# Decoder layers on one core: feed-forward weights split early and parked in DRAM

## The reference

```python
x = x + attention(layernorm(x))             # 16 heads of 64, causal
x = x + cross_attention(layernorm(x), ctx)  # 16 heads of 16, linear: K^T V first, then Q (K^T V)
x = x + ffn(layernorm(x))                   # two layers l = 0, 1, each as below

def ffn_layer(x):
    h = shift_token(x)                      # upper half of the features from the token before
    q, k, v = split(h @ wqkv[l], 3)         # 256 x 1536, 8 heads of 64
    q = rotary(l2norm(q) * q_scale[l]); k = rotary(l2norm(k) * k_scale[l])
    x = x + local_attention(q, k, v) @ wo[l]   # windows of 128, own and previous window
    h = layernorm(shift_token(x)) * ln_g[l] + ln_b[l]
    a, g = split(h @ w1[l] + b1[l], 2)      # 256 x 1364
    return x + (a * gelu(g)) @ w2[l] + b2[l]
```

## Time and profile before

| what | before |
|---|---|
| median of 3 runs (lowest, highest) | 1188.23 us (1187.99, 1189.28) |
| the profiled execution: own time | 1190.71 us |
| the profiled execution: span of its instructions | 1188.9 us |
| granted TensorE clock, mean | 0.995 of full speed |
| busy: TensorE / VectorE / ScalarE / GpSimd | 96% / 69% / 58% / 48% |
| DMA: moved, mean busy share of 16 engines (q1) | 46.14 MB, 13.1% |

### The profile page before, as it was taken

The page is one execution under the profiler, slowest core; times in us unless marked ns, Lnnn a source line. Parts: engine busy times, 40 slices in busy tenths (PEclk is TensorE's granted clock), DMA queues, the critical chain, the costliest instruction groups (busy, mean ns, idle before and its releaser), DMA issues.

```text
span 1188.9 us, 19605 instructions
## 1 busy us (share of the span) xinstructions
PE 1138.9 (96%) x6624; PEld 886.1 (75%) x6624; DVE 816.7 (69%) x2443; ACT 692.5 (58%) x1696; POOL 567.4 (48%) x618
## 2 busy tenths in 40 slices
PE   4999999999999999998989999999999999999998
PEld 3778778787877766766667777777877778777686
DVE  5878778778877456689988566766575765654541
ACT  2677677777677223453676646747565565573821
POOL 2344544444454222148976464655554646561520
PEclk9999999999999999999999999999999999999999
DMA  7122221312121500011030000000001000001010
GB/s 238 41 50 62 56 50 41 80 37 54 41 50 40 174 18 18 1 62 36 2 131 1 1 1 18 2 1 1 1 18 48 27 1 1 1 16 57 18 36 18
DMA packets 30273, 46.14 MB, mean 39 GB/s; under 512 B 4576, under 2 KB 18016, under 8 KB 30176
## 3 DMA queue, kind: packets, MB, share of 16 engines
q1 hardware_dynamic: 30176, 44.90, 13.1%
HBM read 23.92 MB, written 4.19 MB: 24 GB/s over the span
## 4 chain that ended last, share of the span: by engine, by line
PE 86%; DVE 6%; ACT 3%; issue 2%; POOL 1%; DMA 0%; DVEq 0%; ACTq 0%; POOLq 0%
PE psum L1483 53%; PE psum L1572 6%; PE psum L1554 5%; PE psum L1704 5%; PE psum L1753 5%; PE psum L1738 5%; PE psum L1720 4%; PE psum L1686 2%; ACT hnT_hi L955 1%; ACT hnT L955 1%; DVE stats L1027 1%; PE psum L1766 1%; DVE rb L1272 1%; DVE y L1036 0%; DVE ss L1276 0%
## 5 line engine op out<-in xcount | busy, mean ns | idle before, releaser
L688 POOL TENSOR_TENSOR probs<-probs,rden 128x128 f32<-128x128 f32 (+3 forms) x256 | 176.5, 721 | 195.9 <-DVE rden L1094 195.9
L925 ACT ACTIVATE lp<-lp,lneg,rn 128x256 f32<-128x256 f32 (+1 forms) x256 | 143.8, 572 | 20.3 <-DVE lneg L1323 20.1
L837 ACT ACTIVATE probs<-probs,negmax 128x128 f32<-128x128 f32 (+3 forms) x256 | 140.7, 551 | 15.1 <-DVE negmax L1089 14.5
L1082 DVE CUSTOM_DVE_ANT_0 probs<-psum,causal 128x512 f32<-128x512 f32 (+3 forms) x256 | 110.0, 487 | 13.3 <-PE psum L1483 13.3
L727 POOL TENSOR_TENSOR rn<-ssm,neg_half 128x8 f32<-128x8 f32 x64 | 106.1, 1657 | 0.0
L1311 DVE CUSTOM_DVE_ANT_0 lp<-psum,local 128x256 f32<-128x256 f32 (+1 forms) x256 | 84.2, 385 | 22.0 <-PE psum L1704 21.9
L718 POOL TENSOR_TENSOR lp<-lp,lrden 128x768 f32<-128x768 f32 x64 | 94.9, 1483 | 0.0
L1483 PE MATMUL psum<-w,hid 124*128 124x256 f32 (+2 forms) x384 | 87.4, 385 | 2.6 <-DVE hid L1387 2.6
L1554 PE MATMUL psum<-ident,probs 128*128 128x128 f32 x640 | 86.0, 273 | 1.5 <-DVE pT L1103 1.1
L1483 PE MATMUL psum<-q,k_rest 128*128 128x256 f32 (+2 forms) x256 | 85.5, 345 | 1.3 <-DVE rowmax L1082 1.0
L1483 PEld LDWEIGHTS psum<-w,hid 124*128 124x128 f32 (+2 forms) x384 | 73.2, 193 | 14.4 <-issue 4.0
(11 more groups left out here) (167 smaller groups left out, 2982.2 us busy)
## 6 DMA issues: line engine op xcount, KB each, us to landing
k<-k_round SPq DMA_DIRECT2D x128, 128.0 KB, 2.4
x<-in_x SPq DMA_DIRECT2D x8, 512.0 KB, 6.3
aw<-in_w_quads SPq DMA_DIRECT2D x4, 768.0 KB, 4.7
w_raw<-in_w SPq DMA_DIRECT2D x2, 1364.0 KB, 6.4
ctxT<-in_ctxT SPq DMA_DIRECT2D x4, 512.0 KB, 7.3
x_scratch<-x SPq DMA_DIRECT2D x4, 512.0 KB, 2.9
x<-x_scratch SPq DMA_DIRECT2D x4, 512.0 KB, 6.3
wqkv_raw<-in_wqkv SPq DMA_DIRECT2D x1, 1536.0 KB, 10.2
```

The lines of the kernel that those rows point to most:

```text
L688: ins = pool.tensor_tensor(pr, pr, rden[:, u % 2, h, i:i + 1].broadcast_to([P, TRI[i]]), ALU.mult)
L837: ins = act.activation(pr, pr, ACT.Exp, bias=negmax[:, u % 2, h, i:i + 1], scale=ADH ** -0.5, accum_out=den[:, u % 2, h, i:i + 1])
L925: ins = act.activation(pr, pr, ACT.Exp, bias=lneg[:, u % 2, h, w:w + 1], scale=rn[:, m % 2, w, 0, 2 * j + h:2 * j + h + 1], accum_out=lden ...
L1082: ins = dve.tensor_tensor_reduce(probs[:, u % 2, h, TRI_AT[i]:TRI_AT[i + 1]], bank[:, at:at + TRI[i]], causal[:, S - TRI[i]:S], 1.0, -3e38 ...
```

## The change

**Splitting moves into the self-attention units.** All feed-forward weights are laid out on the host as one array `w_all` of 8360 columns a layer by 128 rows (wqkv in three parts, w1, w2, wo). It is cut into 11 parts of 760 columns a layer, 22 in all. In units 4 to 25 each part goes through the same path: SyncE loads it (`load_part`), ScalarE rounds it (`round_part`, item `part` behind `pk`), GpSimd subtracts in place (`rest_of_part`, item `part` behind the second `f`), SyncE stores both halves to a scratch array in DRAM (`store_part`), and waits for the stores before it loads the part after next.

**The halves are read back ready for use.** `layer_wqkv_lo`, `layer_wqkv_hi` and `layer_w1` load both halves from DRAM; `weights`, `w1_parts`, and their VectorE and ScalarE work in entry and steps are gone. TensorE waits for the loads instead. w2 and wo are still loaded unsplit, though their columns are split too.

**Tables.** `tab.0` moves to VectorE's unit 28 and `tab.1` behind the second cross-attention norm; both are stored to DRAM and each layer's one is loaded into a single `tab`, layer 1's after the last q and k tile of layer 0. The buffers of all this lie in `y`, which is free until the cross-attention ends.

**Orders.** `START_*`, `ENTRY_*` and `CLOSE_*` are rewritten on all engines; of these tables the diff shows one pair of lines. The repeated unit differs by the `part` items alone, the step by the missing ones.

```diff
+W_SIZE = (E2 * INNER,) * 3 + (E2 * 2 * HID, NF * D, FPAIRS * D)
+W_AT = [sum(W_SIZE[:i]) for i in range(len(W_SIZE) + 1)]
+W_PARTS = 11
+FIRST_PART = 4
+W_PART = W_AT[-1] // W_PARTS
...
+        w_raw = sbt(raw, "w_raw", [P, 2, W_PART])
+        w_half = sbt(raw, "w_half", [P, 2, W_PART], F32R)
...
+        w_rest = sbt(raw, "w_rest", [P, 2, W_PART], F32R)
...
-        START_PE = ("xT.0 pq.0 pk.0 pv.0 xT.1 s.0.0 s.0.1 pk.1 xT.2 pq.1 pv.1 t.0.0 pv.2 s.1.0 t.0.1 "
+        START_PE = ("xT.0 pv.0 xT.1 pk.0 pq.0 pv.1 s.0.0 s.0.1 pk.1 pq.1 pv.2 t.0.0 t.0.1 xT.2 s.1.0 "
...
-        UNIT_ACT = ("t1 e0@1 pk@2 t3 t5 aw0 pq@2 aw1 e1@1 pv@2 aw2")
-        UNIT_POOL = ("f0@6 f1@6")
+        UNIT_ACT = ("t1 e0@1 pk@2 part t3 t5 aw0 pq@2 aw1 e1@1 pv@2 aw2")
+        UNIT_POOL = ("f0@6 f1@6 part@6")
...
+                if what == "part" and 0 <= n - FIRST_PART < DEPTH * W_PARTS:
+                    items.append((what, n - FIRST_PART))
...
+            def store_part(i):
+                l, c = divmod(i, W_PARTS)
+                sp.wait_ge(part_lo, i + 1)
+                for half, tile in enumerate((w_half, w_rest)):
+                    sp.dma_start(w_dram[l, half, :, c * W_PART:(c + 1) * W_PART], tile[:, i % 2, :].bitcast(F32))\
+                        .then_inc(part_st, 16)
...
+                i = u - FIRST_PART - 2
+                if 0 <= i < DEPTH * W_PARTS:
+                    store_part(i)
+                    if i + 2 < DEPTH * W_PARTS:
+                        sp.wait_ge(part_st, 2 * 16 * (i + 1))
+                        load_part(i + 2)
...
-            wait_early(sp)
+            sp.wait_ge(l_tab, 6 * DEPTH)
+            for l, done in enumerate((tab_first, rot)):
+                sp.dma_start(tab_dram[l], done[:, :, :, :].rearrange("p a t d -> p (a t d)")).then_inc(tab_st, 16)
+            sp.wait_ge(tab_st, 16 * DEPTH)
+            wait_full(sp, plan["awo", B - 1, 1])
+            for c in range(3):
+                layer_wqkv_hi(0, c)
+            wait_read(sp, plan["kv", B - 1, T - 1])
+            layer_tab(0)
...
+            wait_full(sp, plan["q", B - 1, T - 1])
+            layer_wqkv_lo(1, 0)
+            layer_wqkv_hi(1, 0)
...
+            def rest_of_part(i):
+
+                pool.wait_ge(part_hi, i + 1)
+                pool.tensor_tensor(w_rest[:, i % 2, :], w_raw[:, i % 2, :], w_half[:, i % 2, :], ALU.subtract)\
+                    .then_inc(part_lo, 1)
...
-            def round_weights(l):
-
-                act.wait_ge(ld_wqkv, 16 * (1 + 3 * l))
...
+            def round_part(i):
+
+                act.wait_ge(ld_part[i % 2], 16 * (i // 2 + 1))
+                if i >= 2:
+                    act.wait_ge(part_st, 2 * 16 * (i - 1))
+                copy(w_half[:, i % 2, :], w_raw[:, i % 2, :]).then_inc(part_hi, 1)
...
                     if m % B == 0:
-                        pe.wait_ge(w_lo, 3 * l + "qkv".index(what) + 1)
+                        pe.wait_ge(ld_wqkv["qkv".index(what)], 2 * 16 * (l + 1))
```

More of the change, by code:

```diff
@@ L81, in constants, with build @@
             "c_rot": np.ascontiguousarray(rot)}
-def build(nc, a, out, x2_dram):
+def build(nc, a, out, x2_dram, w_dram, tab_dram):
     with ExitStack() as ctx:
@@ L101, in build @@
         k_rest = sbt(raw, "k_rest", [P, 2, S], F32R)
+        w_raw = sbt(raw, "w_raw", [P, 2, W_PART])
+        w_half = sbt(raw, "w_half", [P, 2, W_PART], F32R)
+        raw.close()
+        raw = ExitStack()
+        k_rest_again = sbt(raw, "k_rest_again", [P, 2, S], F32R)
+        w_rest = sbt(raw, "w_rest", [P, 2, W_PART], F32R)
+        raw.close()
+        raw = ExitStack()
+        k_rest_too = sbt(raw, "k_rest_too", [P, 2, S], F32R)
+        rot = sbt(raw, "rot", [P, 4, T, FDH])
+        tab_first = sbt(raw, "tab_first", [P, 4, T, FDH])
+        qk_scale = sbt(raw, "qk_scale", [P, DEPTH, 2, FDH])
         raw.close()
@@ L107, in build @@
         raw.close()
[L108 to L111, removed]
+        wqkv_lo = sbt(ctx, "wqkv_lo", [P, 3, E2, INNER], F32R)
         stats = sbt(ctx, "stats", [P, 2, T, 12])
@@ L210, in build @@
         raw.close()
-        wqkv_hi = sbt(ctx, "wqkv_hi", [P, E2, 3 * INNER], F32R)
+        wqkv_hi = sbt(ctx, "wqkv_hi", [P, 3, E2, INNER], F32R)
         sq = sbt(ctx, "sq", [P, 2, INNER])
-        tab = [sbt(ctx, f"tab{l}", [P, 4, T, FDH]) for l in range(DEPTH)]
-        rot = tab[DEPTH - 1]
-        qk_scale = sbt(ctx, "qk_scale", [P, DEPTH, 2, FDH])
+        tab = sbt(ctx, "tab", [P, 4, T, FDH])
         hT_hi = sbt(ctx, "hT_hi", [P, E2, S + 1], F32R)
@@ L251, in build @@
         x2_st = sem("x2_st")
-        ld_rot, ld_small, ld_wqkv, ld_lwo, ld_w1, ld_w2 = (
-            sem(n) for n in ("ld_rot", "ld_small", "ld_wqkv", "ld_lwo", "ld_w1", "ld_w2"))
+        ld_rot, ld_small, ld_lwo, ld_w1, ld_w2 = (
+            sem(n) for n in ("ld_rot", "ld_small", "ld_lwo", "ld_w1", "ld_w2"))
+        ld_wqkv = [sem(f"ld_w{what}") for what in "qkv"]
+        ld_tab, tab_st = sem("ld_tab"), sem("tab_st")
+        ld_part = [sem(f"ld_part{i}") for i in range(2)]
+        part_hi, part_lo, part_st = sem("part_hi"), sem("part_lo"), sem("part_st")
         set1 = sem("set1")
         ld_shift = sem("ld_shift")
-        w_hi, w_lo = sem("w_hi"), sem("w_lo")
         hid_one, last_gate = sem("hid_one"), sem("last_gate")
-        w1_hi_ok, w1_lo_ok = sem("w1_hi_ok"), sem("w1_lo_ok")
         hn_hi, hn_lo = sem("hn_hi"), sem("hn_lo")
@@ L399, in step_items @@
                     items.append((what, n))
-                if what == "weights" and n == B:
-                    items.append((what, 1))
-                if what == "tab" and n == B:
-                    items.append((what, 1))
-                if what == "wparts" and n % B == 0:
-                    items.append(("w1_parts", n // B))
             return items
@@ L774, in _ @@
                     probabilities(*at)
+                if what == "part":
+                    rest_of_part(*at)
                 if what == "norm2":
@@ L779, in _ @@
                     query_norms(*at)
-                if what == "weights" and at[0] == 0:
+                if what == "zeros":
                     set_zeros()
@@ L938, in evac_O @@
                 copy(loT[:, FPAIRS - 1 - u % FPAIRS, :], bank[:, :]).then_inc(read[use[0]], 1)
-            def split_w1(l):
-                act.wait_ge(ld_w1, 16 * (l + 1))
-                for e in range(E2):
-                    copy(w1_hi[:, e, :], w1_raw[:, e, :]).then_inc(w1_hi_ok, 1)
             def evac_hnT(m):
@@ L996, in _ @@
                     evac_xo(*at)
-                if what == "weights":
-                    round_weights(*at)
-                if what == "w1_parts":
-                    split_w1(*at)
+                if what == "part":
+                    round_part(*at)
                 if what == "hT":
@@ L1229, in tables @@
                 H = FDH // 2
+                dst = (tab_first, rot)[l]
                 for i in range(2):
@@ L1432, in _ @@
                 if what == "y":
+                    if at[0] == 0:
+                        dve.wait_ge(tab_st, 16 * DEPTH)
                     norm_apply(norm_no["y", at[0]], x[:, at[0]], y[:, at[0]])
-                if what == "weights":
-                    rest_of_weights(*at)
-                if what == "w1_parts":
-                    rest_of_w1(*at)
                 if what == "tab":
@@ L1670, in qkv_tile @@
                     if m % B == 0:
-                        pe.wait_ge(w_lo, 3 * l + "qkv".index(what) + 1)
+                        pe.wait_ge(ld_wqkv["qkv".index(what)], 2 * 16 * (l + 1))
                 use = plan[what, m, t]
                 bank = wait_free(pe, use)
-                cols = slice("qkv".index(what) * INNER, ("qkv".index(what) + 1) * INNER)
+                c = "qkv".index(what)
                 rows = slice(t * P, (t + 1) * P)
-                product(bank[:, :], [(h[:, e, rows], w[:, e, cols]) for e in range(E2)
+                product(bank[:, :], [(h[:, e, rows], w[:, c, e, :]) for e in range(E2)
                                      for h, w in ((hT_lo, wqkv_hi), (hT_hi, wqkv_lo), (hT_hi, wqkv_hi))])\
@@ L1898, in by_hidden_tiles, with by_partitions, rows @@
         return tiles
+    def by_partitions(wqkv, w1, w2, wo):
+        def rows(w):
+            w = np.asarray(w)
+            return w.reshape(DEPTH, -1, P, w.shape[-1]).transpose(0, 2, 1, 3).reshape(DEPTH, P, -1)
+        qkv = [rows(np.asarray(wqkv)[..., c * INNER:(c + 1) * INNER]) for c in range(3)]
+        return np.concatenate(qkv + [rows(w1), w2.reshape(DEPTH, P, -1), rows(wo)], -1)
     arrays = {
```

146 lines of the change are left out of this document (71 added, 75 removed), and 89 rows, old and new, of tables (CLOSE_DVE, ENTRY_ACT, ENTRY_DVE, ENTRY_PE).

## The result

| | before | after |
|---|---|---|
| median, us (runs) | 1188.76 (4) | 1203.11 (4) |
| lowest to highest | 1187.99 to 1189.83 | 1201.91 to 1204.84 |
| profiled execution: own time, span | 1190.7, 1188.9 | 1201.95, 1200.2 |

The changed kernel takes 1.0117 times as long, 95% interval 1.0105 to 1.0129. The prediction said 8.7 us faster; it is 14.4 us slower by the medians, 11.3 by the spans of the two profiled executions.

What follows compares the result with a forecast made beforehand. TensorE, busy nearly all the span, was taken as the bound, waiting in the entry for VectorE's chain. Terms -9.0 - 1.6 - 1.0 + 1.1 + 1.8 = -8.7 us gave 1179.5 us from the median of 1188.2, range 1172 to 1189.

Steps and rivals of the forecast that it cites:

- SyncE and DMA: Units: two stores and a load per part between copies of k on SyncE's queue, taken to cost 0.
- Rival 3: Copies of k queue behind the parts on SyncE in each of 22 units: about 1214 us, chance 0.06.
- Entry: Up to 650 us: 7.7 us leaving VectorE taken back, plus 1.3 behind: -9.0 us, bounds 0 and -13.7.
- clock's 1.4: Entry: one window where the granted clock fell to 0.71 would be 1.4 us shorter at full clock.
- Rival 2: GpSimd takes VectorE's place in the entry, only 3 of the 9 us come: 1185.5 us, chance 0.10.
- Tables: Two rotary tables, 2.7 us of VectorE each at most, in their new places: 0, at most +2.
- Units: 22 parts: +1.1 us, ScalarE's copies ending 0.06 ahead of z's start; three units also splitting a quad's weights: +1.8 us.
- Rival 1: Path ScalarE, GpSimd, TensorE late in every unit, 0.4 us each, 8.8 in place of 1.1: 1187.2 us, chance 0.15.
- rival 4: Nine aw_lo in three quad units each held for a whole 1.81 us GpSimd subtraction: 1194 us, chance 0.03.
- Layer 1: Split of layer 1's weights, between steps 1 and 2, replaced by loads: -1.6 us, range 0 to -1.6.
- Start: From 25 to 105 us: pv.0 goes first and fills a wait: -1.0 us, from +2 to -3.7.
- Rival 5: Halves return from DRAM too late for the first q tile, entry's gain gone: 1188.5 us, chance 0.04.

Runs made afterwards that it cites:

- e1: Changed kernel with SyncE's block that stores and loads a part put ahead of the wait for aw_lo and the quad's load: 1190.7 us, 1.0015 times before.
- e6: Changed kernel with the next part's load ahead of the aw_lo wait, then the quad's load, then stores, with no wait for stores just issued: 1193.5 us.
- e7: e5 with the entry's four lists of the kernel before, less the splits' items, both tables behind norm2.1: 1191.9 us.
- e5: Changed kernel with e1's edit and tab.0 moved behind norm2.1: 1189.3 us, ratio 1.0001 to the kernel before.
- e9: e5 with 16 parts (w2, wo unsplit), none in units that split aw, and the close's lists of the kernel before: 1184.4 us, 0.9947 times before.
- e10: e5 with 16 parts (w2, wo unsplit), none in units splitting aw, and the start's old lists, part.0 kept in GpSimd's: 1189.2 us.
- e2: Changed kernel with the quad's load still first, no wait for stores just issued, each part's load one unit later: 1205.3 us.

## Why the prediction was wrong

*SyncE and DMA, "0": this term failed.* Rival 3 had the right mechanism, copies of k queued behind the parts on SyncE, but I set its condition with the times of a plain unit: stores and load between 235.45 and 244.3. In a plain unit that held, stores landed in 2.6 and 3.3 us and loads in 3.1, and no copy of k was late. In the two units with a quad's load the term of the order was missing: SyncE first waits for `aw_lo` until some 2 us before the source of the next copies is ready (114.36 and 116.56), and 768 KB stand ahead of the stores. The stores then took 6.0 and 6.4 us. The low end of that reading, the load landing at 242, has no row behind it; loads of a part landed in 3.1 us. I had costed these units on ScalarE and VectorE only (+1.8, measured +1.5), never on the queue. Price: 12.4 us by e1, of which e6 gives 9.7 to the wait and 2.8 to the bytes. The prediction's own test, "DMA as what it waits for at scores", is what the profile showed.

*Entry, -9.0: right in sign, -5.7 measured.* The step that failed is "I take back the 7.7 us that leave VectorE". Taken out under the old order they gave 1.9 us (e7), 1.1 of it in idle time. A nearly full engine is not the bound if the waits at which TensorE stands are chains through it with gaps elsewhere. I named the new order in half a sentence and gave it nothing; it gave 2.3 in idle time. The "clock's 1.4" came in this execution, partly by luck: three of ten executions with the new lists still have the fall. Rival 2 was partly there: with the old order the wait for GpSimd's rotation grew from 2.5 to 2.9 us, a small part of the 6 us that rival took away, and the new order cut it to 0.5.

*Tables, "0, at most +2": +2.2.* I gave a table "2.7 us of VectorE each at most"; tab.0 took 3.6. "Go where TensorE is gapless and VectorE three quarters busy" was an argument from shares. The place in the list counts: ahead of the copies of t.28, and beside GpSimd's f. Behind norm2.1 the same table takes 1.5 us and costs nothing in the traces (e5).

*Close, "0, within 1 either way": +2.0,* the new order of the close (e9).

*Units, +1.1 and +1.8:* right, +1.2 and +1.5. `w_half` took 826 ns and `w_rest` 1834, against 0.83 and 1.81 us forecast. GpSimd's f was waited for twice, 0.6 us each, in units 14 and 22 only. Rival 1 did not come at its price, but its path was met: z waits 0.07 us for ScalarE's copies in every other plain unit. The "0.06 ahead" was no slack: where z waits, it starts 0.36 us behind the end of those copies.

*The port pair (rival 4): its price did not come in its place, but leaving it without a term was wrong.* The median of aw_lo is 698 ns (688 before). The first aw_lo of each of the three quads took 1.31 or 1.32 us already before (three in twelve, where the prediction counts one), and 1.32, 0.97 and 0.97 after. The rule of the Trainium skill (SBUF — State Buffer, SBUF: two separate sides) fits these and, better, tab.0, whose instructions have two SBUF inputs: 3.6 us beside GpSimd's f instead of 1.5, ahead of what TensorE waits for. In e10 a `negmax` with one SBUF input ends with the subtraction of a part, 1.23 us instead of 0.17, and that costs 1.1. Both are holds on TensorE's path, which the prediction sought at aw_lo alone.

*Layer 1, -1.6:* right. The first hidden products of steps 1 and 2, in the chain of waits of the kernel after, against the earlier trace rows:

```profile
737.77 2.97 PE psum L1512 x12
...
816.10 2.97 PE psum L1512 x12
```

78.3 us apart, where it had been 79.9. *Start, -1.0:* right in size (0.4 to 1.8 by the traces). *Rival 5* did not come: no wait for the layers' halves shows.

The forecast's sum of right terms was thus close where one instruction's duration met one instruction's slack, and off where a place in a queue, or the neighbour on another engine, decided.

## What to carry to other kernels

When a change adds transfers to a queue that also carries something urgent, walk the queue once for every kind of iteration, the rare ones first: write down what it waits for, what stands behind that wait, and when the urgent transfer is due. Put waits that end late behind everything that is ready; here that alone was worth 12.4 us of 1203. Put work whose result nobody needs soon behind what is needed. And count busy time taken off a full engine only where a wait of the bound engine hangs on the very instructions removed: 9.5 us of VectorE's work gave 1.9. Before you take an instruction's duration for a new place, look what GpSimd does beside it there. And before you credit an order with a stretch, compare idle time: a fall of the clock moved this one by 1.5 us with no change in the program.

## What the runs showed of the hardware that I had not expected

A wait of 4.3 us on TensorE cost 6.1, as the granted clock of the next 4 us was 0.57. A wait of 1.15 us (e6) was followed by no such fall: the window from 120 to 125 us stands at 1.00. In e2, where TensorE stood 5.1 us until 123.75, a window shortly behind the wait reads:

```profile
125.00:127.00 2.00, 2.00 (x8) 0.76 (x6) 1.13 (x3) 1.78 (x6) 2.00 (x3) 0.50 0.78 266
```

That is 1.2 GHz throughout. So a stall of 4.3 to 4.9 us in the units was priced at 1.3 to 1.4 times its length, and one of 1.15 us at 1.35 us, near its own.

An instruction of VectorE can take several times its length beside one of GpSimd: a 128x4 `negmax` 1.23 us instead of 0.17 (e10), the rows of a rotary table 1.04 instead of 0.42 (after, e5).
